# A mixture-of-experts tower: GpSimd waits for the landing of a tile's two scatters before it issues the next tile's

## What is computed

```python
logits = xt @ router_w.T + router_b
topk_p, topk_i = lax.top_k(softmax(logits), 2)
gates = sum(one_hot(topk_i) * topk_p[..., None], axis=1)
h = gelu(xt @ w1e.T + b1e); y = h @ w2e.T + b2e        # for each expert e
acc = acc + y * ge[:, None]
```

## Time and profile before

| | |
|---|---|
| median of 3 runs | 673.35 us |
| span of the profiled execution | 771.4 us |
| busy: TensorE, VectorE, ScalarE, GpSimd | 84%, 73%, 64%, 54% |
| DMA | 184 GB/s over the span |
| scatters of `back` (line 1257) | 160, 972 ns each on GpSimd |
| mean granted TensorE clock | 0.957 |

### The profile page before, as it was taken

How to read it: one execution, slowest core, us unless ns; L and a number is a source line. 1 busy time by engine, 2 the same in 40 slices (tenths; PEclk the granted TensorE clock), 3 DMA queues, 4 the chain that set the end, 5 groups by cost and what they waited for, 6 DMA issues and landing times.

```text
span 771.4 us, 24553 instructions
## 1 busy us (share of the span) xinstructions
PE 647.2 (84%) x7952; PEld 594.7 (77%) x7952; DVE 562.3 (73%) x1797; ACT 493.0 (64%) x1259; POOL 413.1 (54%) x446
## 2 busy tenths in 40 slices
PE   4999999999999999988877665878888787888870
PEld 4999999999999999888875554766666666666660
DVE  3877888888888888778886444756565756677777
ACT  4678876766667666554446343657666767777783
POOL 0243344777767666655656646545555555545552
PEclk9999999999999999999997767999999999999995
DMA  8987877888888887765522222344323234444555
GB/s 318 372 263 271 277 253 251 261 267 256 276 261 267 276 244 236 236 213 182 162 64 60 71 63 73 108 123 119 111 78 98 78 93 118 138 137 131 170 177 195
DMA packets 71895, 141.67 MB, mean 184 GB/s; under 512 B 13078, under 2 KB 55650, under 8 KB 63838
## 3 DMA queue, kind: packets, MB, share of 16 engines
q1 hardware_dynamic: 62128, 121.69, 50.1%
q0 software_dynamic: 9280, 17.21, 6.4%
q10 hardware_dynamic: 366, 1.21, 0.5%
HBM read 116.35 MB, written 25.66 MB: 184 GB/s over the span
## 4 chain that ended last, share of the span: by engine, by line
PE 25%; DVE 24%; another core or an unknown queue 13%; issue 13%; ACT 4%; POOL 3%; DMA 1%; POOLq 0%; ACTq 0%; DVEq 0%; SPq 0%
PE pair L1279 14%; DVE patches L1099 7%; PE pair L1434 3%; DVE patches L1121 2%; PE pair L1325 2%; POOL sent L1235 2%; ACT pair L680 2%; PE pair L1452 2%; PE pair L1289 1%; DVE patches L1114 1%; DVE h L1172 1%; DVE patches L1107 1%; DVE patches L1132 1%; DVE field L843 1%
## 5 line engine op out<-in xcount | busy, mean ns | idle before, releaser
L1257 POOL DMA_INDIRECT back<-patches x160 | 157.0, 981 | 150.6 <-DVE patches L1114 104.6
L680 ACT ACTIVATE pair<-pair,b1s 128x256 f32<-128x256 f32 x320 | 126.3, 448 | 110.4 <-remote 51.5
L1279 PE MATMUL pair<-field,patches 128*128 128x128 f32 (+1 forms) x1408 | 173.9, 280 | 8.9 <-DMA patches<-in_x 8.6
L1279 PEld LDWEIGHTS pair<-field,patches 128*128 128x128 f32 (+1 forms) x1408 | 164.6, 194 | 9.6 <-issue 8.6
L1235 POOL DMA_INDIRECT sent<-pay,slot_own x130 | 149.2, 1148 | 40.3 <-issue 38.2
L1434 PE MATMUL pair<-patches,ex_hi 128*128 128x256 f16 x640 | 119.4, 280 | 47.8 <-DVE patches L1099 23.8
L605 ACT ACTIVATE gate<-pair,lbias 128x128 f32<-128x128 f32 x260 | 74.4, 369 | 98.1 <-PE pair L1294 88.6
L1452 PE MATMUL pair<-ex_hi,patches 128*128 x1280 | 117.4, 225 | 8.3 <-issue 6.1
L1247 POOL TENSOR_TENSOR rstd<-veps,cst 128x2 f32<-128x2 f32 (+1 forms) x68 | 58.0, 853 | 107.2 <-DVE veps L800 106.6
L1107 DVE CAST patches<-pair 128x256 f16<-128x256 f32 x80 | 33.7, 422 | 109.6 <-remote 105.2
L1434 PEld LDWEIGHTS pair<-patches,ex_hi 128*128 x640 | 56.6, 99 | 72.8 <-issue 64.0
(11 more groups left out here) (150 smaller groups left out, 1257.7 us busy)
## 6 DMA issues: line engine op xcount, KB each, us to landing
patches<-in_x SPq DMA_DIRECT2D x62, 1152.0 KB
patches<-sent SPq DMA_DIRECT2D x80, 130.0 KB
field<-in_we SPq DMA_DIRECT2D x64, 128.0 KB
field<-back SPq DMA_DIRECT2D x10, 768.0 KB
patches<-in_b SPq DMA_DIRECT2D x80, 64.0 KB
field<-in_pos SPq DMA_DIRECT2D x65, 64.0 KB
out_tower<-h SPq DMA_DIRECT2D x10, 384.0 KB
back<-patches POOLq DMA_INDIRECT x160
```

Source lines behind the costliest of these rows:

```text
L680: last = act.activation(up[:, cols], up[:, cols], ACT.Gelu, bias=b1s[:, bass.ds(e * FC + 2 * half + i, 1)], scale=1.0 / E_SCALE)
L1257: pool.indirect_dma_start(back, bass.IndirectOffsetOnAxis(ap=dsti[j % NO][:, k:k + 1], axis=0), yo[j % NO][:, k, :], None, bounds_check=2 ...
L1279: last = pe.matmul(bank_of, l, w_, start=(c == KS and k == 0), stop=(c == KS - 1 and k == 2))
```

## The change

Before GpSimd issues the two scatters of tile j it now also waits until both scatters of tile j-1 have landed: its semaphore must have reached 32 times the number of tiles that used that ring buffer. Nothing else changes: the same instructions run in the same order on every engine.

```diff
                 if 0 <= j <= TILES_B - 1:
                     through(pool, dst_done, j)
                     through(pool, y_done, j)
+                    if j >= 1:
+                        pool.wait_ge(y_out[(j - 1) % NO], ((j - 1) // NO + 1) * 16 * HALVES)
                     for k in range(HALVES):
                         pool.indirect_dma_start(back, bass.IndirectOffsetOnAxis(ap=dsti[j % NO][:, k:k + 1], axis=0),
                                                 yo[j % NO][:, k, :], None, bounds_check=2 * TOKENS - 1,
```

## The result

The changed kernel takes 847.94 us (median of 4 runs) against 673.33: a ratio of 1.261, 95% interval 1.256 to 1.267. The direction was right; the size wasn't: 783 was forecast, with a range up to 835.

The account below looks back on a forecast made before the run. GpSimd's chain of issues, landing and restart was taken to bound the kernel: tile 8's start at 435, 5 for early waits, 71 x 4.3, 21 for chunk loads, 1.28, 2.11 and 12.8 gave 783 us; range 725 to 835.

Parts of the forecast that it names:

- The new bound: Expert part: GpSimd's chain of issue, landing and restart becomes the bound, above TensorE's 3.13 us for a tile.
- link: GpSimd, one tile's first scatter to the next's: two issues, landing, restart; 4.3 us, bounds 3.7 and 5.0.
- The end of the tail: After tile 79's first scatter: 1.28 us issue, 2.11 landing and an unchanged 12.8 us to the end.
- Which landing: A tile's second scatter: quiet landing of 2.11 us taken, upper bound 2.9 beside the 130 KB row loads.
- the chunk loads: Nine loads of `back` in the loop delay scatters issued behind them: 9 x 2.3 = 21 us, bounds 0 and 42.
- The seam: Tiles 0 to 8, among 14 other scatters: only tiles 3, 4, 5 and 8 pay 1.17 us each, about 5 us.
- The timed period: Expert part before the change: a timed run takes 3.13 us for a tile, against 3.84 in the trace.
- The first rival: Expert part: the stalls are the chip's, timed runs have the 3.84 us period too; 727 us, chance 0.12.
- SyncE's stops: SyncE's waits at steps 52 and 74: up to 34 us at step 52, both costed at nothing.
- the second rival: Expert part: TensorE's clock falls to half for half the tiles, 855 us; sign: clock below 0.8; chance 0.06.
- The 911 us of the rule weighed: Landings in the loop: 2 us HBM latency at high load would add 128 us; weighed, not adopted.
- the extremes of a link with all loads in the way: GpSimd's chain with all bounds high: 5.0 us for each link, 42 us for loads of `back`; 853 us, outside the range.

Follow-up runs that it names:

- e6: Changed kernel without the bias loads from tile 4 on (biases of the first four tiles used again), row loads kept; 814.68 us.
- e3: Changed kernel, from tile 4 on loading only the two tag columns of the sorted rows (2 KB for 130 KB) and no bias row; 810.09 us.
- the second profile: The kernel before the change, with no edit, profiled once more; 677.41 us, span 675.6.
- e9: Changed kernel with each tile's bias load reading 128 different 512-byte rows of the input images, same bytes and pieces; 820.05 us.

## Why the prediction was wrong

- **The new bound: right for most of the way.** GpSimd's chain of issue, landing and restart sets the end, but for 37 and 14 us behind SyncE's stops. 1.28, 2.12 and 0.85 us were read rightly for a quiet landing at the end of the program; within the loop a quiet one is 2.24 and the link 4.37. The end of the tail, 16.2 us from tile 79's first scatter, came out at 845.7 - 829.73 = 16.0.
- **Which landing: wrong, 38 us.** "I take **4.3**" for a link, with 21 us for the chunk loads, made 326 us; 71 links measured 364. The same 71 links take 337.9 us in e6 (462.89 to 800.78) and 329.0 in e3 (461.96 to 790.92). So 26 of the 38 us are the bias load, some 9 the rows in place of the tags, and 3 the rest, by one profile each (the two runs of e6 lie 8 us apart). The 329.0 us of e3 are 71 x 4.37 and 19 more for chunk loads and stops, where 21 were forecast: that term held. The quiet value was taken because the 130 KB load would be through in time. That was nearly so. The term had priced loads by their bytes and left out the 64 KB bias load as the smaller. Its upper bound for the landing, 2.9 us, is a little under what the loop showed on average, 3.0: the choice between the bounds went to the wrong end.
- **The seam: wrong, 25 us.** Tile 8 was put at 435 + 5 and started at 465.4. Of this 19 us come from counting back from the end with TensorE's period: GpSimd was already behind at tile 8, which the second profile of before shows (454.05). The text had the 14 scatters and their 1.28 us each, and used them only as cover for the waits. The other part is that the early waits cost 465.4 - 454.0 = 11 us and not 5: the text counted each as 4.3 - 3.13, but GpSimd, being behind, would have issued a tile every 2.55 us there. They can't be caught up as GpSimd has no slack left.
- **Together.** 783 + 38 + 25 = 846, and 2 us lie outside the span.
- **The timed period: near.** 3.13 us from TensorE's busy time; the second profile gives 2.9. The first rival (stalls of the chip) is refuted by it.
- **SyncE's stops: nothing in sum, but not for the reason given.** SyncE waited for landings 96.6 us in all, at most 33.4 at a time (34 were forecast). That "the cover is that stock of finished tiles" failed: after both stops GpSimd stood for results that TensorE and VectorE hadn't made yet, and tile 54 started at 702.11, an estimated 5 us later than six links of 5.08 from tile 48 (666.33) would give. In return, links beside a standing SyncE take 4.37 us and not 5.08, which gives back an estimated 5 us in the seven links of the first stop.
- **The clock.** It fell where TensorE had little or nothing to do, in and behind SyncE's two stops, and came back to 0.91 between them (the stretches, in the columns of the earlier trace rows):

```profile
636.00:665.00 29.00, 2.82 (x36) 2.51 (x36) 3.80 (x8) 2.71 (x6) 13.09 (x14) 0.64 0.09 29
...
700.00:760.00 60.00, 43.48 (x490) 37.44 (x488) 36.19 (x84) 39.32 (x86) 21.57 (x22) 0.91 0.34 104
760.00:780.00 20.00, 0.00 (x0) 0.00 (x0) 1.04 (x4) 0.00 (x0) 8.63 (x10) 0.50 0.06 14
780.00:830.00 50.00, 13.32 (x160) 11.48 (x160) 20.89 (x53) 16.55 (x42) 19.98 (x21) 0.64 0.31 100
```

  From 480 to 830 us its mean is 0.82, above the 0.8 that would have spoken for the second rival. It cost a little in the refill: the first twelve matmuls of line 1436 on the chain after the first stop take 2.70 us, later ones 1.3 to 1.5. In its last links GpSimd is released by landings, not by VectorE.

The range failed with it. Its high end left out "the extremes of a link with all loads in the way", and that was the case: 5.08 us from tile 20 to 40 is above even the high bound of a link, 5.0. The 911 us of the rule weighed were not reached; the landing grew by 0.8 us and not by 1.8.

## What to carry to other kernels

When a wait for a DMA's landing is put between two issues of one queue, price the link as issue, landing beside the loop's real traffic, and restart, and compare it with the pace of the busiest engine; the rest of the kernel then follows this chain. Don't price the neighbours of a transfer by bytes: here a small broadcast that reads one short row for every partition cost the scatters more than a load of twice its size. Leave out each neighbour in turn, with as few pieces left as can be, and not only double one: a doubled load is a new neighbour, and it moves those queued behind it.

## What the runs showed of the hardware

- A load that reads one 512-byte row of `b2` 128 times lengthens the landing of a 64 KB scatter beside it from a median of 2.2 us to 3.1. A load of 128 different rows of the images, with the same bytes and pieces, lengthens it by 0.2 (e6, e9, after).
- GpSimd's restart after a landing takes 0.85 us to the start of the next scatter, against 0.30 between two scatters that wait for nothing.
- A profiled execution can be 96 us longer than another of the same kernel: 771.4 against 675.6 us of span. A second profile, or the busy time of the engine that is full, shows it.
